# A transformer of four blocks on one core: the second attention's first steps placed in the experts' last ones, and local attention's keys ahead packed for two heads

## Time and profile before

| what | value |
|---|---|
| runs, us | 1659.86, 1664.57, 1665.05; median 1664.57 |
| profiled execution, us | 1666.25 |
| its span, us | 1664.5 |
| mean granted TensorE clock | 0.96 of full speed |
| TensorE busy | 1522.5 us (91%) |
| TensorE weight loads | 1044.9 us (63%) |
| VectorE busy | 1142.5 us (69%) |
| ScalarE busy | 1078.2 us (65%) |
| GpSimd busy | 518.7 us (31%) |
| DMA, mean | 22 GB/s |

### The profile page before, as it was taken

How to read it: one execution, slowest core, us unless ns; L and a number is a source line. 1 busy time by engine, 2 the same in 40 slices (tenths; PEclk the granted TensorE clock), 3 DMA queues, 4 the chain that set the end, 5 groups by cost and what they waited for, 6 DMA issues and landing times. The chain is left out here.

```text
span 1664.5 us, 30601 instructions
## 1 busy us (share of the span) xinstructions
PE 1522.5 (91%) x10286; PEld 1044.9 (63%) x10286; DVE 1142.5 (69%) x2344; ACT 1078.2 (65%) x2475; POOL 518.7 (31%) x476
## 2 busy tenths in 40 slices
PE   7999999999979999999969999996998888899986
PEld 5777777777667888888844333333666655566664
DVE  2666666666658777777768888854777753767755
ACT  2555555555567888888836777744777754777752
POOL 1222222222232111222110000015767623776632
PEclk9999999999979999999987999967999998999999
DMA  7000000000011221222100000000000000000000
GB/s 235 2 2 0 0 0 0 0 0 0 2 50 55 77 76 64 74 76 76 38 0 1 1 1 1 1 1 1 1 1 1 1 1 1 1 1 1 1 2 26
DMA packets 18994, 36.37 MB, mean 22 GB/s; under 512 B 5764, under 2 KB 11008, under 8 KB 16704
## 3 DMA queue, kind: packets, MB, share of 16 engines
q1 hardware_dynamic: 18896, 35.09, 6.3%
HBM read 33.91 MB, written 1.18 MB: 21 GB/s over the span
## 5 line engine op out<-in xcount | busy, mean ns | idle before, releaser
L904 DVE TENSOR_TENSOR m_hidp<-m_hid,m_hidp 128x512 fp32r<-128x512 f32 x256 | 178.6, 724 | 76.3 <-ACT m_hidp L826 75.5
L305 ACT ACTIVATE a_prob<-ps,a_negmax 128x512 f32<-128x512 f32 (+3 forms) x256 | 133.8, 525 | 146.7 <-DVE a_negmax L381 146.7
L831 ACT ACTIVATE m_hid<-ps,pre_w 128x512 f32<-128x512 f32 x256 | 175.2, 685 | 61.8 <-PE ps L1040 61.3
L1095 PE MATMUL ps<-m_hidp,m_w2p 128*128 128x512 f32 x768 | 192.1, 399 | 0.0
L1387 DVE TENSOR_REDUCE c_sb_negmax<-ps 128x1 f32<-128x512 f32 x256 | 162.5, 683 | 38.7 <-PE ps L1529 38.5
L1040 PE MATMUL ps<-m_xp,m_w1p 128*128 128x512 f32 x768 | 188.9, 395 | 0.0
L1311 ACT ACTIVATE c_sb_pT<-ps 128x512 f32<-128x512 f32 x256 | 137.4, 601 | 73.1 <-PE ps L1544 72.2
L265 POOL TENSOR_TENSOR a_qk_r<-a_qk_c,a_qk_s 128x512 f32<-128x512 f32 x64 | 81.3, 1270 | 325.3 <-DVE a_qk_s L372 325.3
L1925 ACT ACTIVATE l_sb_prob<-ps,l_sb_negmax,l_sb_rn 128x192 f32<-128x192 f32 (+1 forms) x256 | 124.0, 494 | 77.4 <-DVE l_sb_negmax L2029 77.3
L1040 PEld LDWEIGHTS ps<-m_xp,m_w1p 128*128 128x128 f32 x768 | 144.9, 189 | 36.4 <-issue 3.0
L1095 PEld LDWEIGHTS ps<-m_hidp,m_w2p 128*128 128x128 f32 x768 | 145.5, 190 | 35.2 <-issue 0.3
(11 more groups left out here) (228 smaller groups left out, 3173.1 us busy)
## 6 DMA issues: line engine op xcount, KB each, us to landing
m_gate_all<-m_gates_d SPq DMA_DIRECT2D x16, 1024.0 KB, 4.7
pre_w<-w1T SPq DMA_DIRECT2D x14, 258.0 KB, 2.7
pre_w<-w2T SPq DMA_DIRECT2D x14, 256.0 KB, 2.8
pre_wqkv<-wqkv SPq DMA_DIRECT2D x2, 768.0 KB
keep_x<-x SPq DMA_DIRECT2D x1, 1024.0 KB, 9.3
out<-keep_x SPq DMA_DIRECT2D x4, 256.0 KB, 2.3
keep_xT<-xT SPq DMA_DIRECT2D x1, 768.0 KB, 5.1
pre_m_w<-l_w SPq DMA_DIRECT2D x2, 341.0 KB
```

What stands on the lines that cost most here:

```text
L305: nc.scalar.activation(prob[:, u % 4, 0:width(p)], score_ps(b, p, j)[:, 0:width(p)], ACT.Exp, bias=negmax[:, u:u + 1], accum_out=den[:, b ...
L831: nc.scalar.activation(hid[:, c % 2, f, :], ps[:, f, :], ACT.Gelu, bias=w1[:, k, FF + f:FF + f + 1]).then_inc(gelu_done, 1)
L904: nc.vector.tensor_tensor(hidp[:, c % 2, 1, f, :], hid[:, c % 2, f, :], hidp[:, c % 2, 0, f, :], ALU.subtract).then_inc(low_done, 1)
L1095: ins = nc.tensor.matmul(ps[:, 4 + c % 2, :], w2p[:, k, a, f, :], hidp[:, c % 2, b, f, :], start=(f == 0 and i == 0), stop=(f == FB - 1 an ...
```

## The change

The diff does two things.

*First*, a new class `Head` holds the first steps of the second attention, for quad 0 its q and k products, its eight units of maxima and its split and turned shift, and for quad 1 its q and k products. Its tiles and semaphores live across both blocks. `experts0` calls these steps behind its last expert's, woven into the end of the block in an order written out by hand on TensorE, ScalarE and VectorE. The experts' `xp` becomes the same buffer as the second attention's `st`. In `experts0` the two first batches are turned back earlier (`turn_x` in steps 1 and 2), `finish_norm(0)` stands in step 2 behind the remainders, and `turn_fin` no longer stands ahead of the last down-products. The banks change (`X_TURN`, `FIN_TURN`). The head takes the maxima of two banks in one instruction. In `attention1` what is left before the first exponential is `project(2, 0)` and units 8 to 10; `project(2, 1)` goes behind the first unit of exponentials, with its `leading` and `remain`. The rotary `tables` go from VectorE's start of `layers` to its quad 2. Two memsets (`shp`, `oneb`) go from GpSimd's start of `layers` to its start of `experts0`.

*Second*, in local attention a pair of heads lies in 384 columns, `[own 0 | ahead 0, ahead 1 | own 1]`, in the keys, the mask, the scores' banks, `prob` and `probT`. `turn_p` turns three blocks of 128, and the copies take 384 columns. The middle block, turned, has head 0's 64 keys ahead in rows 0 to 63 and head 1's in rows 64 to 127. The previous tile's values for head 1 stand in rows 64 to 127 already. Those for head 0 are copied by ScalarE to rows 0 to 63 of a new tile `v_low`, whose other rows are zero, one more copy (64 x 256) in each tile but the last of a batch.

```diff
@@ -861,15 +866,21 @@
         def step(n, e, k, c, last):
             if not (last and c == NB - 1):
                 gelus(n + 1, (c + 1) % NB, (k + (c + 1) // NB) % 2)
-            if last and c >= 1:
+            if last and c in (1, 2):
                 copy_x(c - 1)
-            if last and c >= 2:
-                copy_fin(c - 2)
 
         each_step(act, step)
-        copy_x(NB - 1)
-        copy_fin(NB - 2)
-        copy_fin(NB - 1)
+        copy_fin(0)
+        copy_x(2)
+        head.leading(act, 0, 0)
+        head.leading(act, 0, 1)
+        copy_x(3)
+        copy_fin(1)
+        head.leading(act, 1, 0)
+        copy_fin(2)
+        head.leading(act, 1, 1)
+        copy_fin(3)
+        head.copy_shift(act)
 
...
         def step(n, e, k, c, last):
             if not (last and c == NB - 1):
                 lows(n + 1, (c + 1) % NB)
+            if last and c == 2:
+                finish_norm(0)
...
         each_step(dve, step)
-        finish_norm(NB - 2)
-        second_moments(NB - 1)
-        finish_norm(NB - 1)
+        second_moments(2)
+        finish_norm(1)
+        head.remain(dve, 0, 0)
+        head.remain(dve, 0, 1)
+        second_moments(3)
+        finish_norm(2)
+        head.maxima(dve, 0)
+        head.maxima(dve, 1)
+        finish_norm(3)
+        head.remain(dve, 1, 0)
+        head.maxima(dve, 2)
+        head.maxima(dve, 3)
+        head.remain(dve, 1, 1)
+        for k in range(4, 8):
+            head.maxima(dve, k)
+        head.shift(dve)
...
             ins.then_inc(down_mm, 1)
             if isinstance(n, int) and n < NB:
                 bias_down(c)
-            if last and c >= 1:
+            if last and c in (1, 2):
                 turn_x(c - 1)
-            if last and c >= 2:
-                turn_fin(c - 2)
+
+        def first_products(w):
+
+            pe.wait_ge(gelu_done, FB * (STEPS - 1) + w + 1)
+            head.project(pe, 0, w)
 
         each_step(pe, step)
-        turn_x(NB - 1)
-        turn_fin(NB - 2)
-        turn_fin(NB - 1)
+        turn_fin(0)
+        turn_x(2)
+        pe.wait_ge(fin_ev, 1)
+        first_products(0)
+        first_products(1)
+        turn_x(3)
+        pe.wait_ge(x_ev, 3)
+        head.project(pe, 1, 0)
+        turn_fin(1)
+        pe.wait_ge(gelu_done, FB * STEPS)
+        head.max_scores(pe, 0)
+        head.max_scores(pe, 1)
+        turn_fin(2)
+        head.max_scores(pe, 2)
+        head.max_scores(pe, 3)
+        head.project(pe, 1, 1)
+        turn_fin(3)
+        for k in range(4, 8):
+            head.max_scores(pe, k)
+        head.turn_shift(pe)
...
+class Head:
...
+    def bank(self, k, i):
+
+        return (0 if k % 2 else 2) + i
+
+    def project(self, pe, m, w):
+        pre = self.keep["pre"]
+        if m and w:
+            pe.wait_ge(self.st_done, 3)
+        self.nc.tensor.matmul(self.product(m, w), (pre.wq, pre.wk)[w][:, m * P:(m + 1) * P],
+                              self.keep["xT"][:, 0, :], start=True, stop=True).then_inc(self.qk_mm, 1)
+
+    def max_scores(self, pe, k):
+        if k == 0:
+            pe.wait_ge(self.st_done, 2)
+        for i in range(2):
+            g = 2 * (k % 2) + i
+            r = slice(32 * g, 32 * g + 32)
+            if k >= 2:
+                pe.wait_ge(self.max_done, 2 * (k - 1))
+            self.nc.tensor.matmul(self.ps[:, self.bank(k, i), :], self.st[r, 0, 0, (k // 2) * P:(k // 2 + 1) * P],
+                                  self.st[r, 1, 0, :], start=True, stop=True).then_inc(self.max_mm, 1)
...
+    def remain(self, dve, m, w):
+        dve.wait_ge(self.lead_ev, 2 * m + w + 1)
+        c = (2 * w + 1) * NB
+        self.nc.vector.scalar_tensor_tensor(self.st[:, w, m, :], self.product(m, w), self.keep["pre"].rot[:, c:c + 1],
+                                            self.lead[:, w, :], ALU.mult, ALU.subtract).then_inc(self.st_done, 1)
+
+    def maxima(self, dve, k):
+        g = 2 * (k % 2)
+        dve.wait_ge(self.max_mm, 2 * k + 2)
+        self.nc.vector.tensor_reduce(self.negmax[:, 0, k // 2, g:g + 2],
+                                     self.ps[:, self.bank(k, 0):self.bank(k, 0) + 2, :], AX.X, ALU.max, negate=True
+                                     ).then_inc(self.max_done, 2)
+
+    def shift(self, dve):
+        dve.wait_ge(self.max_done, 16)
+        dve.wait_ge(self.shp_zero, 1)
+        self.nc.vector.tensor_copy(self.shp[:, :, :, 0], self.negmax[:, 0, :, :]).then_inc(self.sh_step, 1)
+        dve.wait_ge(self.sh_step, 1)
+        self.nc.vector.tensor_tensor(self.shp[:, :, :, 1], self.negmax[:, 0, :, :], self.shp[:, :, :, 0], ALU.subtract
+                                     ).then_inc(self.sh_step, 1)
...
-        remain(0, 0)
-        remain(0, 1)
-        maxima(0)
-        maxima(1)
-        remain(1, 0)
-        maxima(2)
-        maxima(3)
-        remain(1, 1)
-        maxima(4)
-        maxima(5)
+        maxima(8)
         remain(2, 0)
-        maxima(6)
-        maxima(7)
-        shift_lead(0)
-        remain(2, 1)
-        shift_remain(0)
-        for k in range(8, AHEAD):
-            maxima(k)
+        maxima(9)
+        maxima(10)
         for m in range(NQ - 1):
             k = m * NUNIT + AHEAD
             maxima(k)
+            if m == 0:
+                remain(2, 1)
             maxima(k + 1)
             if m and m + 2 < NQ:
                 remain(m + 2, 1)
+            if m == 2:
+                tables()
...
-        project(0, 0)
-        project(0, 1)
-        pe.wait_ge(ones_set, 1)
-        max_scores(0)
-        max_scores(1)
-        project(1, 0)
-        max_scores(2)
-        max_scores(3)
-        project(1, 1)
-        max_scores(4)
-        max_scores(5)
         project(2, 0)
-        max_scores(6)
-        max_scores(7)
-        project(2, 1)
-        max_scores(8)
-        max_scores(9)
-        turn_shift(0)
-        max_scores(10)
+        for k in range(NUNIT, AHEAD):
+            max_scores(k)
         for m in range(NQ):
             for r in range(NUNIT):
                 e = m * NUNIT + r
                 exp_scores(e)
                 if e + AHEAD < ALL:
                     max_scores(e + AHEAD)
+                if m == 0 and r == 0:
+                    project(2, 1)
...
         def copy_v(n, t):
             act.wait_ge(v_mm, n + 1)
+            if layer == 0 and n == 0:
+                act.wait_ge(inited, 4)
+            if t + 1 < TPB:
+
+                wait_past(act, o_mm, n - 2)
+                nc.scalar.activation(v_low[0:WIN, t, :, :],
+                                     v_ps(n)[WIN:P, :].rearrange("p (m i c) -> p m i c", m=2, i=2)[:, :, 0, :],
+                                     ACT.Copy).then_inc(low_ev, 1)
             nc.scalar.activation(v[:, t, :], v_ps(n), ACT.Copy).then_inc(v_ev, 1)
...
         def turn_p(n, t, k):
             pe.wait_ge(exp_done, PAIRS * n + k + 1)
             wait_past(pe, pT_ev[k % 2], 2 * n + k // 2)
-            for i in range(2):
-                for a in range(0 if t else 1, 2):
-                    ins = nc.tensor.transpose(ps[:, 4 + k % 2, (2 * i + a) * P:(2 * i + a + 1) * P],
-                                              prob[:, k % 2, i, a * P:(a + 1) * P], ident[:, :])
+            for a in range(0, 3, 1 if t else 2):
+                ins = nc.tensor.transpose(ps[:, 4 + k % 2, a * P:(a + 1) * P], prob[:, k % 2, a * P:(a + 1) * P],
+                                          ident[:, :])
             ins.then_inc(pT_mm, 1)
...
+            if t and m == 0:
+                pe.wait_ge(low_ev, n - n // TPB)
             for i in range(2):
-
-                for a in range(1, -1 if t else 0, -1):
-                    for j in range(2):
-                        u = head(2 * m + j, i)
-                        ins = nc.tensor.matmul(o_ps[64 * j:64 * j + 64, (u // 2) * P:(u // 2 + 1) * P],
-                                               v[:, (t + a - 1) % TPB, u * HD2:(u + 1) * HD2],
-                                               probT[:, j, i, a * P:(a + 1) * P], start=(a == 1),
-                                               stop=(a == 0 or t == 0), skip_group_check=True)
+                for j in range(2):
+                    u = head(2 * m + j, i)
+                    ins = nc.tensor.matmul(o_ps[64 * j:64 * j + 64, (u // 2) * P:(u // 2 + 1) * P],
+                                           v[:, t, u * HD2:(u + 1) * HD2], probT[:, j, 2 * i * P:(2 * i + 1) * P],
+                                           start=True, stop=(t == 0), skip_group_check=True)
+                for j in range(2 if t else 0):
+
+
+                    u = head(2 * m + j, i)
+                    r = slice(WIN * i, P)
+                    ahead_v = v[r, t - 1, u * HD2:(u + 1) * HD2] if i else v_low[:, t - 1, m,
+                                                                                 j * HD2:(j + 1) * HD2]
+                    ins = nc.tensor.matmul(o_ps[64 * j:64 * j + 64, (u // 2) * P:(u // 2 + 1) * P], ahead_v,
```

(1 more changed line is left out.)

197 lines of the change are left out of this document (109 added, 88 removed).

## The result

| | time, us | ratio to before | 95% interval |
|---|---|---|---|
| before | 1664.88 (8 runs, 1659.86 to 1666.73) | 1 | |
| after | 1655.89 (8 runs, 1651.36 to 1658.24) | 0.9953 | 0.9940 to 0.9966 |
| forecast | 1651 (1643 to 1658) | 0.992 | |

The kernel became faster by 9.0 us by the medians (7.8 by the ratio), where 13.5 were forecast. The same kernel run a second time (e7_again) gave 1654.64, ratio 0.9927 (0.9909 to 0.9945), 10.7 by the medians and 12.2 by the ratio. Of the two intervals, in us, the first (5.7 to 10.0) leaves out 13.5 and the second (9.2 to 15.2) holds it.

The account below looks back on a forecast made before the run. No single bound: TensorE in the experts' steps, a seam of some 39 us that hardly fills one engine, a ring of waits in local attention. 8.5 + 5.0 = 13.5 us off the median 1664.57 gives 1651, range 1643 to 1658.

Parts of the forecast that it names:

- The last down-product: End of the experts: no longer queued behind the normalised tile, it runs 844.7 to 847.7 instead of ending at 852.1.
- VectorE's list: Head: moments, normalisations, remains, maxima and shift operations in order take 19.3 us, to 868.9, plus a wait of 0.4.
- The block change: From the head's end to the next block's first product: costs its 1.02 us again, to 871.6.
- the key product behind the first unit: Second attention, quad 2's key product on TensorE: taken as cold, 1.83 us, leaving 9.5 gained at the third unit.
- Tables and memsets: Rope tables among a later quad's maxima cost 0.7 us (0 to 1.4); two memsets at GpSimd's experts start cost 0.3.
- Part 2: Local attention, keys ahead packed: 0.35 less 0.14 for the form change, 0.21 us per tile, 24 tiles: 5.0 us.
- Rival (c): Local attention: each form change drains, 0.38 us a pair against 0.35 saved, so packing gives nothing: 1656; chance 0.17.
- rival (e): Second attention's first quads: TensorE's clock stays down, some 1.4 us more per unit, 16 units make 1673; chance 0.04.
- The sign that I had set for (e): Second attention: TensorE's granted clock at 0.50 more than 8 us after the first unit.
- (a): Whole kernel: both parts work, the form change takes a third of the packing's gain: 1651, 1648 to 1655; chance 0.46.
- test set in advance: Whole kernel: the forecast is wrong if the two parts in the trace miss 8.5 and 5 by over 2 us each.
- (b): Whole kernel: form change free, double maxima cheaper, tables in slack, clock back for the moved key product: 1645.4; chance 0.25.

Follow-up runs that it names:

- e7_again: The changed kernel run once more with no edit, for a second profile and more runs: 1654.64 us, ratio 0.9927.
- e12_before_fill: The kernel before, with three unread 128x512 bf16 products in unit 6 of quads 2 to 14: 1659.90 us, ratio 0.9952.
- e3: The changed kernel with the rope tables put back at VectorE's start of the last block: 1654.69 us, ratio 0.9943.
- e4_rows: The changed kernel with the second head's ahead product on all 128 rows, no form change, output not the reference's: 1649.07 us, ratio 0.9902.
- e1_head: The kernel before with the first part of the change only (head beside the experts), local attention as before: 1659.77 us, ratio 0.9979.
- e5_late2: The changed kernel with the second attention's first product held back some 1.9 us behind a memset of v1: 1656.08 us, ratio 0.9948.
- e9_fill: The changed kernel with three unread 128x512 bf16 products in unit 6 of quads 2 to 14: 1644.43 us, ratio 0.9865.
- e2_pack: The kernel before with the second part of the change only (packed keys ahead), head and tables as before: 1660.65 us, ratio 0.9978.
- e11_end: e9_fill with nine more unread products ahead of the first transposition of normalised tiles in quad 14: 1641.62 us, ratio 0.9856.

## Why the prediction was right, and where it was short

**The last down-product** ran 844.45 to 847.52, forecast 844.7 to 847.7. Right. A part of its old 4.57 was luck, though: in e12_before_fill, which has the old order there, it took 3.04 (846.10), and from the last down-product but one to the third unit that profile takes 49.66, so between the two filled kernels the seam is worth 8.1 and not 9.6.

**VectorE's list.** 19.3 us to 868.9, plus a wait of 0.4, head end 870.6: measured 867.87 and, with the copy of the shift, 869.2. The double maxima gave 0.6 over eight (1.16 to 1.18 each), inside the bounds; the gates were done 0.36 earlier (849.24). Right within 1.4, of which 0.3 is that the whole seam stood 0.28 earlier.

**The block change** of 1.02 came again (869.17 to 870.19), and the key product behind the first unit ran cold (2.08), as taken. Forecast at the third unit 9.5, measured 9.6 and 9.75. That it fits so closely is partly luck: the head ended 1.1 earlier than forecast, counted from the last down-product but one, and two stretches behind it were longer, by 0.5 from the block's first product to the first exponential's scores (3.64 against 3.15) and by 0.5 from there to the third unit (8.75 against 8.27).

**Tables and memsets.** The tables cost 1.35 of VectorE's time (913.01 to 914.36) where 1.4 was the estimate; whether any of it is on the path isn't shown (e3). The 0.3 for the memsets is not there: on GpSimd the first deviation follows the memset of `m_ones` by 1.42 (459.92 to 461.34), where it was 1.34 (462.17 to 463.51) before. They lie in a wait, 0.1 at most.

**Part 2.** Per tile 0.35 - 0.14 = 0.21: measured 0.21 on two tiles of four, with the 0.14 shown by itself in e4_rows. The two layers together gain 4.7, against 5.0. That sum needed the other two tiles of a batch to come to 0.22 together (-0.14 and 0.36), which the forecast did not work out: there it was lucky. Rival (c), a cost of 0.38 for each pair, did not come; it would have left no gain.

**The sum** failed in a term that it did not have. I weighed the clock as one event, rival (e): will it come back after the head? It did, by the third unit, as before. I gave it a chance of 0.04 and otherwise let the quads stand at their old length. But four of before's own quads already had a stretch at half clock (three pitches of 15.7 and one of 16.9, against 14.19), and the windows that I weighed end at 896. The quad time is not a constant; from 204.0 it went to 207.6 and 212.9 with the change, to 205.7 with the tables back, and stayed at 203.6 in e1_head and e5_late2. In the two profiles of after it took back 8.8 and 3.5 of the seam's gain, and 3.0 and 1.0 came back behind it. That is most of what these two profiles (8.0 and 10.0 shorter than before's) lack to 13.5. What remains is mostly 1.6 in the last MLP, one more stretch at half clock in every profile of a kernel that has the packing (last add to end 52.4 to 53.2) and in none of before, e1_head and e12_before_fill (51.5); its cause is open.

Nor do I know what starts a stretch in the quads: the wait in unit 6 is part of it, since filling it ends them, but the same wait is there in the quads that run at full clock. The sign that I had set for (e), a granted clock of 0.50 more than 8 us after the first unit, did come (0.50 from 892 to 896 in after, the first unit at 873.83), but it is no sign of this rival: before has it too (0.50 from 944 to 946, the first unit at 886.05).

So the mechanisms of (a) are shown, and a small part of (e) with them: the seam's gain and the packing's by the traces, the clock's share by the windows of after and by the fill, in size only roughly. By the test set in advance, 8.5 and 5 in the trace within 2 us each, both parts held up to the third unit and in the layers; in the runs part 1 alone gave 3.5. The range, 1643 to 1658, held the time because it had been drawn for (c), which did not happen; the 1648 to 1655 of (a) would have missed 1655.89. That is luck. The chances have a slip: (a), (b) and (c) make 0.88, so "something taken off" can't leave 0.89.

## What to carry to other kernels

Before a gain in one stage is added to the time, look whether the stages behind it run at one clock: compare the pitch of a repeated unit through the whole stage (14.19, 15.7, 18.8 here) rather than its mean. Where some repeats are longer with the same instructions, price that as a range of its own, take a second profile, and try a few unread products in TensorE's longest regular wait; it costs a few lines and gave about as much here (8 to 15 us by the ratios) as the change under study (8 to 12).

A change of row form inside a chain of small products can be read beforehand from start-to-start gaps. Here 0.14 us was forecast and 0.14 measured.

## What was not expected of the hardware

Thirty-nine unread bf16 products of 128x512, about 0.2 us each (2.12 for nine), took 10 to 11 us by the medians, 10 to 15 by the ratios, off a kernel of 1655 (e9_fill against e7_again and after). TensorE was 92% busy before that, in the stage too (3.16 to 4.00 of 4 us), and its granted clock fell to 0.50 all the same. The same program gave quad times of 212.9 and 207.6 in two profiles, and within some kernels the time of a run goes with its mean granted clock: the correlation is -0.90 over the 12 runs of e1_head, -0.91 over 11 of e2_pack and -0.97 over the 12 of e12_before_fill. It is weak in others (-0.56 over the eight of after, -0.39 over six of e7_again, -0.25 over six of e3_tables) and absent in e11_end (0.14 over five).
